# A causal mask moved into spare contraction rows, with the first two heads' exponents issued earlier

## The reference

```python
x = x + gat(layernorm(x), adj, W, a)          # softmax over neighbours, then probabilities @ (x W)
x = x + mamba2_block(layernorm(x), ...)
x = x + relation(layernorm(x), adj, weight, bias)
x = x + experts(layernorm(x), gate, w1, b1, w2, b2)
```

```python
dt = softplus(dt + dt_bias);  A = -exp(A_log)
A_cum = cumsum(dt * A)                                  # falls along the nodes
Lmat[l, s] = exp(A_cum[l] - A_cum[s]) if s <= l else 0
Y_diag[l] = sum_s (C[l] . B[s]) * Lmat[l, s] * dt[s] * x[s]
```

## Time and profile before

| | us |
|---|---|
| median of 3 runs | 3507.71 |
| lowest, highest | 3505.94, 3511.5 |
| profiled execution, device time | 3515.14 |
| its span in the profile | 3513.2 |
| TensorE matmul busy | 3396.7 |
| VectorE busy | 2532.4 |
| GpSimd busy | 1788.3 |
| ScalarE busy | 1723.9 |

### The profile page before, as it was taken

One profiled execution on the slowest core, in us unless ns is written; L12 is line 12 of the kernel. 1 busy time (PEld: TensorE's weight loads), 2 busy tenths in 40 slices (PEclk: granted clock), 3 DMA queues, 4 the chain that ended last, 5 costly groups with the idle time before them and its releaser, 6 DMA issues.

```text
span 3513.2 us, 62394 instructions
## 1 busy us (share of the span) xinstructions
PE 3396.7 (97%) x19338; PEld 2783.3 (79%) x19338; DVE 2532.4 (72%) x7349; ACT 1723.9 (49%) x3690; POOL 1788.3 (51%) x2043
## 2 busy tenths in 40 slices
PE   7999999999999999999999999997799999999998
PEld 6777777777777777777777777776688888888887
DVE  4888888888888888888888888886344444444444
ACT  3655655655655665655656556554233322333322
POOL 2455455555455555455555555554455554555553
PEclk8999999999999999999999999999899999999999
DMA  3111111111111111111111111110455555556653
GB/s 124 40 37 52 39 36 51 39 36 51 39 36 45 45 36 50 40 36 51 39 42 48 36 51 39 38 50 22 143 194 199 192 192 198 191 192 200 194 191 129
DMA packets 168166, 304.67 MB, mean 87 GB/s; under 512 B 38000, under 2 KB 140400, under 8 KB 149936
## 3 DMA queue, kind: packets, MB, share of 16 engines
q0 software_dynamic: 38272, 196.98, 16.4%
q1 hardware_dynamic: 92880, 72.41, 7.2%
q10 hardware_dynamic: 36960, 34.62, 3.4%
HBM read 250.77 MB, written 53.17 MB: 87 GB/s over the span
## 4 chain that ended last, share of the span: by engine, by line
PE 91%; issue 3%; DVE 3%; ACT 1%; POOL 1%; another core or an unknown queue 1%; DMA 1%; ACTq 0%; DVEq 0%; SPq 0%; POOLq 0%
PE bank L1165 14%; PE bank L1437 14%; PE bank L1451 14%; PE bank L1181 12%; PE bank L1282 7%; PE bank L1396 6%; PE bank L1381 5%; PE bank L1174 4%; PE bank L1363 3%; PE bank L1313 2%; PE bank L1235 2%; PE bank L1304 1%; DVE x L1004 1%; PE bank L1209 1%; PE bank L1403 1%
## 5 line engine op out<-in xcount | busy, mean ns | idle before, releaser
L767 ACT ACTIVATE decay<-bank,w_up 128x256 f32<-128x256 f32 x568 | 268.8, 473 | 701.2 <-PE bank L1437 695.4
L1165 PE MATMUL bank<-xn1T,w_in 128*128 128x256 f32 x2304 | 524.0, 382 | 7.0 <-issue 5.9
L1181 PE MATMUL bank<-w_rel,hT 128*128 128x264 f32 x2048 | 523.5, 394 | 0.0
L1437 PE MATMUL bank<-zs,w_up 128*128 128x256 f32 x2272 | 504.9, 381 | 0.6 <-ACT zs L623 0.6
L1451 PE MATMUL bank<-w_dn,decay 128*128 128x256 f32 x2272 | 502.1, 379 | 0.0
L1165 PEld LDWEIGHTS bank<-xn1T,w_in 128*128 128x128 f32 x2304 | 432.6, 190 | 65.6 <-issue 9.4
L1437 PEld LDWEIGHTS bank<-zs,w_up 128*128 128x128 f32 x2272 | 433.6, 191 | 60.4 <-issue 0.9
L1451 PEld LDWEIGHTS bank<-w_dn,decay 128*128 128x128 f32 x2272 | 426.2, 190 | 55.1
L1113 DVE TENSOR_TENSOR hT<-bank,w_dn 128x256 f32<-128x256 f32 x142 | 60.2, 424 | 537.0 <-PE bank L1451 537.0
L847 DVE SCALAR_TENSOR_TENSOR conv<-bank,conv_w,conv 128x255 f32<-128x255 f32 (+2 forms) x960 | 425.9, 477 | 20.8
L1181 PEld LDWEIGHTS bank<-w_rel,hT 128*128 128x128 f32 x2048 | 364.0, 190 | 80.0 <-issue 24.2
(11 more groups left out here) (238 smaller groups left out, 6166.0 us busy)
## 6 DMA issues: line engine op xcount, KB each, us to landing
token_rows<-row SPq DMA_DIRECT2D x64, 266.0 KB, 3.0
xT_sb<-in_xT ACTq DMA_DIRECT2D x64, 256.0 KB
x_sb<-in_x ACTq DMA_DIRECT2D x64, 256.0 KB, 3.0
adj_sb<-in_adj SPq DMA_DIRECT2D x64, 256.0 KB, 3.5
adjt_sb<-in_adjT SPq DMA_DIRECT2D x64, 256.0 KB, 3.6
out<-row SPq DMA_DIRECT2D x64, 256.0 KB, 2.4
w_in<-token_rows,idc POOLq DMA_INDIRECT x142
out<-hT,ids POOLq DMA_INDIRECT x142
```

The lines of the kernel that those rows point to most:

```text
L767: nc.scalar.activation(hid(f), bank[f % 4][:, 0:GROUP], ACT.Relu, bias=b1[q % 2][:, f:f + 1]).then_inc(hid_ready, 1)
L1165: ins = mm(dst, w_in[:, k, first:first + P], xn1T[:, k, :], start=k == 0, stop=k == DK - 1)
L1181: ins = mm(bank[6 + t][:, 0:GX], hT[:, d, r * N + t * P:r * N + (t + 1) * P], w_rel[:, r, d, :], start=r == 0 and d == 0, stop=r == R - 1 ...
L1437: ins = mm(bank[f % 4][:, 0:GROUP], w1[i][:, k, f * P:(f + 1) * P], xgT[:, k, :], start=k == 0, stop=k == DK - 1)
```

## The change

What it does:
- The masks (L1209) go. `cs3`, `sel` and `selneg` are read in 32 rows per group instead of 24. The rows that a head group doesn't use carry marks: the cumulative sum gets a tile of `factors` and a start value of 1, so that such a row is near zero before its column and 1 from it on, and `selneg` holds -2^60 in these rows for the columns before the mark. This pushes all but the entries in the same block of four nodes far below zero.
- What is left above the diagonal is handled behind: `weigh` takes the minimum with 1 (a cap on values that would be above it) and multiplies by g, and g is now written by VectorE as C.B times `causal`, a tile of ones and zeros, instead of being copied by ScalarE.
- The exponentials are taken for two heads in one instruction, out of two neighbouring banks; heads use banks 2, 3, 4, 5. C.B moves to bank 3, the turned xs to banks 4 and 5.
- `expo(range(0, 4))` is split: heads 0 and 1 stand in front of `relate(1, range(0, 2))`, heads 2 and 3 where all four stood. ScalarE's first pair of exponentials stands in front of the copy of probT.
- More set-up at the start on VectorE and GpSimd.

```diff
 # expo, TensorE
-                    elif h in (2, 3):
-                        pe.wait_ge(xdt_ready, 2 * b + h - 1)
-                    else:
-                        pe.wait_ge(decay_ready, 8 * b + h - 3)
-                    mm(bank[EXPO[h % 4]][:, :].rearrange("p (s l) -> p s l", s=T)[:, :, 0:P], identb[:],
-                       negmask[:].unsqueeze(1).broadcast_to([P, T, P]), start=True, stop=True)
+                    elif h % 2 == 0:
+                        pe.wait_ge(decay_ready, 4 * b + h // 2 - 1)
+                    q, u = h % 4, h // 4
+                    mm(bank[EXPO[q]][:, 0:N], sel[32 * q:32 * q + 32, u, :], cs3[32 * q:32 * q + 32, :],
+                       start=True, stop=False, skip_group_check=True)
+                for h in heads:
+                    q, u = h % 4, h // 4
+                    mm(bank[EXPO[q]][:, N:TRI], sel[32 * q:32 * q + 32, u, :], cs3[32 * q:32 * q + 32, P:N],
+                       start=False, stop=False, skip_group_check=True)
...
 # step, TensorE
+                if b2_ is not None:
+                    expo(range(0, 2), b2_)
                 if b3_ is not None:
                     if b1_ is not None:
                         pe.wait_ge(z_ready, b1_ + 1)
                     relate(1, range(0, 2))
...
-                    expo(range(0, 4), b2_)
+                    expo(range(2, 4), b2_)
...
 # ScalarE
+            def exponentials(j, b):
+                act.wait_ge(expo_made, 8 * b + 2 * j + 2)
+                if j == 0:
+                    need(act, y_made, 2 * b)
+                nc.scalar.activation(decay[:, 2 * j:2 * j + 2, :], expo_banks[j % 2][:, :, 0:TRI],
+                                     ACT.Exp).then_inc(decay_ready, 1)
...
 # VectorE
-                    dve.wait_ge(decay_ready, 8 * b + 2 * j + 2)
-                    v.tensor_tensor(decay[:, 2 * j:2 * j + 2, :], decay[:, 2 * j:2 * j + 2, :],
-                                    g[:, 0:TRI].unsqueeze(1).broadcast_to([P, 2, TRI]), ALU.mult).then_inc(m_ready, 1)
+                    dve.wait_ge(decay_ready, 4 * b + j + 1)
+                    v.scalar_tensor_tensor(decay[:, 2 * j:2 * j + 2, :], decay[:, 2 * j:2 * j + 2, :], 1.0,
+                                           g[:, 0:TRI].unsqueeze(1).broadcast_to([P, 2, TRI]), ALU.min,
+                                           ALU.mult).then_inc(m_ready, 1)
...
-                    ch2.link(dve, v.tensor_tensor_scan(cs[:], ones_row[:], dA[:], 0.0, ALU.mult, ALU.add), b2_)
+                    ch2.link(dve, v.tensor_tensor_scan(cs[:], factors[:], dA[:], 1.0, ALU.mult, ALU.add), b2_)
...
                 if b2_ is not None:
+                    dve.wait_ge(g_made, b2_ + 1)
+                    v.tensor_tensor(g[:], bank[3][:, 0:GW], causal[:], ALU.mult).then_inc(g_ready, 1)
                     dve.wait_ge(g_ready, b2_ + 1)
```

More of the change, by code:

```diff
@@ L97, in sem @@
             return ctx.enter_context(nc.semaphore(name))
-        bank = [ctx.enter_context(nc.psum_tensor(f"bank{i}", [P, 512], F32)) for i in range(6)]
-        bank67 = ctx.enter_context(nc.psum_tensor("bank67", [P, 2, 512], F32))
-        bank += [bank67[:, i, :] for i in range(2)]
+        banks = ctx.enter_context(nc.psum_tensor("bank", [P, 8, 512], F32))
+        bank = [banks[:, i, :] for i in range(8)]
         rows_d = nc.dram_tensor("token_rows", [NT, ROW], F32, kind="Internal").ap()
@@ L456, in _ @@
                 gp.memset(a[:], v)
[L457 to L458 removed]
+            gp.memset(causal[:], 1.0)
             gp.memset(identf[:], 0.0).then_inc(built, 1)
             pool.wait_ge(built, 1)
[L461 to L462 removed]
+            gp.affine_select(identf[:], identf[:], [[-1, P]], ALU.not_equal, 1.0, base=0, channel_multiplier=1)
             gp.affine_select(triub[:], onesb[:], [[1, P]], ALU.is_ge, 0.0, base=0, channel_multiplier=-1)
[L464 removed]
+            for first in (0, N):
+                gp.affine_select(causal[:, first:first + P], causal[:, first:first + P], [[1, P]], ALU.is_ge, 0.0, base=0,
+                                 channel_multiplier=-1)
             gp.iota(row_no[:], [[0, 1]], base=0, channel_multiplier=1)
+            gp.iota(place_no, [[0, T], [1, P]], base=0, channel_multiplier=0, allow_small_or_imprecise_dtypes=True)
             gp.iota(base[:], [[CAP, E]], base=0, channel_multiplier=0, allow_small_or_imprecise_dtypes=True)
@@ L712, in step @@
                     need(act, x1_ready, b1_)
+                    copy(x[:, :, D:GX], banks[:, 0:T, GX + 2:WS])
                     for t in range(T):
-                        copy(x[:, t, D:GX], bank[t][:, GX + 2:WS])
                         ins = nc.scalar.activation(wh[:, t, :], bank[t][:, 0:GX], ACT.Copy, scale=rstd[0][:, t:t + 1])
@@ L717, in step @@
                 nc.scalar.preload_act_table(ACT.Exp)
[L718 to L721, removed]
                 if b1_ is not None:
@@ L731, in step @@
                 if b2_ is not None:
[L732 to L736, removed]
+                    for j in range(1, H // 2):
+                        exponentials(j, b2_)
                 if b1_ is not None:
@@ L1028, in step @@
                     need(dve, rows_out, 16 * b3_)
[L1029 removed]
+                    ins = v.tensor_tensor(row[:, :, 0:GX], banks[:, 6:8, 0:GX], x2b[:], ALU.add)
                     ins.then_inc(x3_ready, 1)
@@ L1213, in expo @@
                         q, u = h % 4, h // 4
[L1214 to L1220, removed]
+                        ins = mm(bank[EXPO[q]][:, first:first + width], cs3[32 * q:32 * q + 32, s:s + P],
+                                 selneg[32 * q:32 * q + 32, u, 0:width], start=False, stop=True,
                                  skip_group_check=True)
```

72 lines of the change are left out of this document (53 added, 19 removed).

## The result

The changed kernel takes 3597.59 us (median of 4 runs, 3594.08 to 3602.05) against 3508.36 us of the kernel before on the same chip (4 runs, 3505.94 to 3511.5). The ratio is 1.0248 [1.0236, 1.0261]: 89 us slower. Forecast were 3506 us and a range up to 3526. The profiled execution after has a span of 3592.2 us, 79 longer than the one before; it is one of the four runs (3594.08 us).

What follows compares the result with a forecast made beforehand. TensorE, busy 97% of the span, was taken as the bound. Masks saved, added call and changed waits summed to 0.06 us a pair, 2 us over 32 pairs: 3506 us from a median of 3507.71, range 3474 to 3526.

Steps and rivals of the forecast that it cites:

- Set-up: Ahead of the loop: about 20 small VectorE instructions, covered by a 3.98 us wait, cost 0, or under 1 us once.
- three signs of being wrong: Two-head calls under 0.3 us, capped product above 1.1 us, or wait for g above 0.7 us in either round.
- Four heads without masks: An expo call on TensorE takes 0.54 us instead of 0.98, its 0.10 us entry gap staying.
- rival 1: Calls shorter: two heads cost half, entry gap goes with the masks; 3490 us, far end 3473; chance 0.31.
- The wait for probT: Before attention, TensorE newly waits 0.30 us; probT comes 0.84 us behind the transposes, a gain of 0.14 us.
- Product g: VectorE's product of C.B and the causal tile behind nmax, 400 columns, takes 0.57 us, interpolated.
- The added call: Expo for heads 0 and 1 before the relation rows costs TensorE 0.62 us in B, 0.86 in A (slots round).
- VectorE's cap and ScalarE's pairs: Minimum plus product in one instruction costs 0 extra (dear end 29 us); a pair's exponents take about 0.83 us.
- rival 2: Slower: VectorE becomes the bound at head 1's bank, 0.25 us a round, 16 us: 3522, dear cap 3535; chance 0.20.
- The pair of rounds: Round B loses 0.05 us, round A gains 0.11: 0.06 us gained a pair, 2 us over 32 pairs.
- TensorE never stands still: In round B (no slots on VectorE) TensorE has no wait; only A stands 0.40 us before L1174.
- rival 3: ScalarE's unexplained pauses at the exponents, 24.1 us in six places, decide: 12 us either way, 3494 or 3518; chance 0.07.

Runs made afterwards that it cites:

- e1: The changed kernel with 25 tiny VectorE memsets in front (loop start 586), against the kernel before: ratio 0.9914.
- e11: The changed kernel with 103 memsets in front (loop start 664, 128 behind the kernel before's 536), against the kernel before: 3487.05 us, ratio 0.9909.
- e5: The kernel before with 50 memsets in front and only the early heads 0 and 1 added, masks kept; against the kernel before: ratio 1.0062.
- e4: The changed kernel with 25 memsets in front, without the early heads (heads 0 to 3 in one call again), against the kernel before: ratio 0.9915.
- e6: The kernel before with 50 memsets in front (loop start 586) and nothing else, against the kernel before: ratio 0.9970.
- e7: The kernel before with 153 memsets in front (loop start 689), one execution timed: 3596.63 us against 3519.1 for the kernel before.
- e2: The kernel before with 25 memsets in front (loop start 561, as in the changed kernel), against the kernel before: ratio 1.0274.

## Why the prediction was wrong

**The step that failed** is the term **Set-up**: about 20 small instructions on VectorE, covered by a wait of 3.98 us, "so 0; if the cover is short, under 1 us once". Their run time is indeed nothing. What I did not price is that every instruction ahead of a loop moves the loop in the engine's list. In place of 0 this term is over +100 us: 27 jumps of 3.8 us (round A to B: median 40.75 us after, 36.93 in e1 and e11) are 103, and by the ratios of the whole kernel (1.0248 against e11's 0.9909) it is near 120. Five of the 25 instructions belong to the product g and not to the set-up. By the blocks above the 20 alone, a start at 556, would have been enough and the five alone, at 541, not; that is an estimate, neither was run. None of the rivals held the step, the slower one neither: that put VectorE's lateness at head 1's bank and at 16 to 29 us. (Its last figure is also mis-added: 3522 and the cap's 29 us are 3551, not 3535.) Nor did any of the three signs of being wrong appear: two heads took over 0.3 us, the capped product under 1.1 us, and the longest wait of TensorE for g in the list above is 0.7 us, while the time went near 72 us past the range. The profile before shows no fetch in the loop; that this hangs on the loop's place, only a padded kernel could have shown.

The other steps can be read in e1, which has the change without the stall. Its TensorE in round A:

```profile
1618.83 1.09 PE L1354 MATMUL bank<-identf,xs 128*128 128x128 f32 x8
1619.86 0.28 PE L1251 MATMUL bank<-cs,sel 32*128 32x256 bf16 x1
...
1620.69 2.05 PE L1222 MATMUL bank<-w_rel,hT 128*128 128x264 f32 x8
1622.57 0.60 PE L1381 MATMUL bank<-identf,prob 128*128 128x128 f32 x4
1623.10 0.28 PE L1251 MATMUL bank<-cs,sel 32*128 32x256 bf16 x2
...
1623.86 2.05 PE L1406 MATMUL bank<-wh,probT 128*128 128x264 f32 x8 [0.25 <-ACT probT L630]
1625.84 0.29 PE L1251 MATMUL bank<-cs,sel 32*128 32x256 bf16 x4
...
1626.28 1.16 PE L1222 MATMUL bank<-w_rel,hT 128*128 128x264 f32 x4
```

and in round B:

```profile
1655.76 1.09 PE L1354 MATMUL bank<-identf,xs 128*128 128x128 f32 x8
1656.79 0.28 PE L1251 MATMUL bank<-cs,sel 32*128 32x256 bf16 x2
...
1657.22 2.05 PE L1222 MATMUL bank<-w_rel,hT 128*128 128x264 f32 x8
...
1662.81 1.16 PE L1222 MATMUL bank<-w_rel,hT 128*128 128x264 f32 x4
1663.80 2.02 PE L1215 MATMUL bank<-w_gc,xT_sb 128*128 128x274 f32 x8
```

- Four heads without masks: 0.44 us from the first L1251 (1625.84) to L1222 (1626.28), as forecast. With the entry of 0.10 us, which stays though the masks are gone (L1406 to L1251 is 1.98 us, where L1363 to the mask was 1.88), that is 0.54. Two heads take 0.43 (1656.79 to 1657.22), as long as four. Right, and it speaks against rival 1.
- The wait for probT: forecast 0.30 us and 0.84 behind the transposes; measured 0.25, and 0.86 behind the transposes, which end 0.10 us of entry before 1623.10 (1623.86 less 1623.00). Right.
- Product g: forecast 0.57 us for 400 columns; the row says 0.57:

```profile
1619.56 0.17 DVE L1002 TENSOR_SCALAR nmax<-emax 128x2 f32<-128x2 f32 x1
1619.64 0.57 DVE L1016 TENSOR_TENSOR g<-bank,causal 128x400 f32<-128x400 f32 x1
```

- The added call: forecast 0.86 in A, 0.62 in B. The transposes of xs in front of it take 0.92 us by the timeline before (this row's start to the first of the earlier trace rows, 1603.65):

```profile
1602.73 1.09 PE L1313 MATMUL bank<-identf,xs 128*128 128x128 f32 x8
```

  Less 0.92, the call is 0.94 us in A (1620.69 less 1618.83) and 0.54 in B (1657.22 less 1655.76). In this round B TensorE doesn't wait for g; in A it does, until the product above ends at 1620.21. The forecast was a little cheap in A, a little dear in B.
- VectorE's cap and ScalarE's pairs, part 5 of the page after, beside the earlier trace rows:

```profile
L892 DVE SCALAR_TENSOR_TENSOR decay<-decay,g 128x768 f32<-128x768 f32 x256 | 252.0, 1014 | 70.1 <-ACT decay L648 68.2
L648 ACT ACTIVATE decay<-bank 128x768 f32<-128x768 f32 x256 | 199.6, 806 | 143.9 <-PE bank L1258 131.4
```

  1014 ns against 1022 for the plain product: the cap is free, and rival 2's dear end falls. A pair of exponents takes 0.81 us, forecast 0.83.
- TensorE's busy time: forecast some 20 us lower; it is 3383.2 us in e1 and 3378.3 in e11 against 3396.7, so 14 and 18 lower.
- The pair of rounds: forecast 0.06 us gained, measured 0.37 (36.46 + 36.93 in e1 and e11, 36.65 + 37.11 before). The step that was mis-sized is round B's "TensorE never stands still". Its relation rows ahead of L1174 take 1.13 us and L1174 2.02 (medians over the loop of the kernel before; the first as in the earlier trace rows); in e1 the same two steps take 0.99 and 1.95, as they do in e5 in both rounds. So 0.21 us of round B were waiting, which the profile doesn't name. Its rows show it: in B L1174 starts 0.16 us after the end of x (1609.78 and 0.89, 1610.83), as close as in A (1646.88 and 0.89, 1647.92), where it does wait. The early heads bring x forward and take that wait in B; in A of e1 x still ends only 0.15 us before the step starts. In e4, without them, the relation rows take 1.24 in one round and 2.13 in the other. Against that stands the added call of 0.54 and 0.94 us, so e4 and e1 come out nearly alike: e4's rounds are 0.23 us a pair shorter (36.93 + 36.23), some 7 us, which the pauses described next hide in the total.
- Luck: without the failed term the kernel would have stood near the 3490 us of rival 1 (see below), but not for rival 1's reason, since its calls aren't shorter than forecast.

**What is left open.** 0.37 us in 28 pairs are 10 us, and e11's rounds are 34 us shorter than before (2326.5 against 2360.6 from the first C.B product to the last). Some 21 us of the rest lie in a few single rounds with a pause of some 3 to 9 us in ScalarE's exponents, the pauses of rival 3: what such rounds take beyond the usual length adds up to 27.1 us in the profile before and 6.1 in e11. It varies between kernels that differ by padding alone (27.1, 33.9, 23.7, 19.2 and 10.4 us for starts 536, 546, 576, 586, 596), one profile each, and runs of one kernel on one chip lie up to 17 us apart too, so whether it belongs to the kernel or to the execution isn't shown. One pause, near 255 to 260 us, has instruction packets beside it; those behind 300 us have none. That padding of 50 and 60 gives 0.9970 and 0.9957 goes with this. I don't know the cause, and so can't say which part of e11's 0.9% is the change's: at equal starts it is 0.9914 / 0.9970 = 0.9944 (e1 over e6, on different chips), about 20 us, and that is the safer figure. By that, the forecast without the failed term was some 17 us too dear, inside its range of 3474 to 3526.

## What to carry to other kernels

A loop has a place and a length in its engine's instruction list; set-up code that costs no time can still push it over a block boundary, and the price is paid at each jump back. Before any edit is judged, compare the instruction packets of the DMA queues before and after: a count that rose by a multiple of the iterations (here 27 x 5) says that part of the time measured comes from the loop's place and not from the edit's own work. Then shift the loop with a few empty instructions, on both kernels, and compare again; or keep the loop short enough to fit at any place, which wasn't tried here.

## What the runs showed of the hardware

- VectorE's list comes in packets of 8.2 KB, and a loop of 279 instructions runs without a fetch from starts 536, 546, 576, 586 and 596 but fetches 5 packets at each jump from 561 and 689; one of 281 runs free from 586 and 664 and fetches from 561. This fits room for four blocks of 128, of which one is fetched ahead: three blocks touched fit, four don't. The block size in instructions is an estimate; that the pattern returns after 128 instructions is measured (561 and 689 fetch).
- Such a jump costs VectorE 3.8 us (103.7 us in 27 places), and TensorE in turn 2.5 us of waiting and over 1 us through the granted clock, which fell to about 0.8 (mean of 4 us) behind the idle stretch. For the whole kernel that is 2.2% (e7), 2.7% (e2) and 3.4% (changed kernel over e11).
- Two row groups of 32 rows take as long as four: 0.43 us against 0.44.
- A minimum with a constant and a product in one instruction on VectorE costs what the product costs: 1014 against 1022 ns for 768 columns.
